# Router logits taken from the attention output by linearity, and the overflow test read from the softmax sums

## What is computed

```python
x = x + _L0_conv_ref(_gn(x), ...)        # linear attention, 8 heads of 32
t = t + _L1_attn_ref(_ln_t(t), ...)      # softmax attention, 8 heads of 32
t = t + _L1_ffn_ref(_ln_t(t), ...)       # experts chosen by a Sinkhorn router
# in _L1_attn_ref
scores = einsum('bhnd,bhmd->bhnm', q, k) / sqrt(Dh)
attn = softmax(scores, axis=-1)
out = einsum('bnd,ed->bne', sa, w_agg) + b_agg
# in _L1_ffn_ref, on batches folded to 4 x 4096 in shape only
gate_logits = einsum('bhnd,hde->bhne', xh, gate_weight)    # 8 numbers a token
gates = _sinkhorn(gate_logits)           # log(clip(logits, 1e-6)), 8 rounds
vals, idx = top_k(g_t, m)                # the best 128 tokens of each expert
```

## Time and profile before

| | us |
|---|---|
| median of 3 runs | 1469.12 |
| lowest, highest | 1467.42, 1470.44 |
| profiled execution, span from the first to the last instruction | 1467.7 |
| PE busy in it | 1339.3 |
| DVE busy | 1021.3 |
| ACT busy | 868.7 |
| POOL busy | 562.6 |

### The profile page before, as it was taken

One profiled execution on the slowest core, in us unless ns is written; L12 is line 12 of the kernel. 1 busy time (PEld: TensorE's weight loads), 2 busy tenths in 40 slices (PEclk: granted clock), 3 DMA queues, 4 the chain that ended last, 5 costly groups with the idle time before them and its releaser, 6 DMA issues.

```text
span 1467.7 us, 29142 instructions
## 1 busy us (share of the span) xinstructions
PE 1339.3 (91%) x10849; PEld 915.8 (62%) x10849; DVE 1021.3 (70%) x2114; ACT 868.7 (59%) x1268; POOL 562.6 (38%) x1068
## 2 busy tenths in 40 slices
PE   5789989999999999999999999999998999987535
PEld 3556656667576767676767676656666567766423
DVE  3536766858585857586768676787789776899771
ACT  2456557677667767677666767665675667542100
POOL 1132530445134513551245214520554116875443
PEclk9899989999999999999999999999999999999665
DMA  2051013600360037002710272005500265454322
GB/s 79 29 137 51 1 30 87 172 16 27 80 184 15 2 93 193 18 2 75 184 46 2 57 168 79 2 30 117 144 15 2 65 169 191 128 158 134 118 68 80
DMA packets 66785, 119.13 MB, mean 81 GB/s; under 512 B 10705, under 2 KB 46546, under 8 KB 66642
## 3 DMA queue, kind: packets, MB, share of 16 engines
q1 hardware_dynamic: 57682, 90.48, 22.9%
q0 software_dynamic: 8960, 26.75, 6.0%
HBM read 29.11 MB, written 33.55 MB: 43 GB/s over the span
## 4 chain that ended last, share of the span: by engine, by line
PE 62%; DVE 24%; issue 6%; POOL 4%; ACT 3%; DMA 0%; DVEq 0%; POOLq 0%; ACTq 0%
PE shared L938 30%; PE scores L894 12%; PE acc L916 11%; DVE prob_sum L1635 6%; PE acc L913 3%; PE shared L933 3%; DVE acc_sb L1609 2%; DVE bn L1344 2%; ACT probs L1209 2%; DVE work L1543 1%; PE acc L926 1%; DVE resid L1350 1%; DVE best_i L1541 1%; DVE best L1539 1%; DVE bn_x L1404 1%
## 5 line engine op out<-in xcount | busy, mean ns | idle before, releaser
L1209 ACT ACTIVATE probs<-scores 128x1024 f32<-128x1024 f32 x512 | 516.0, 1024 | 178.1 <-PE scores L894 94.0
L894 PE MATMUL scores<-query_stack,key_stack 96*128 96x256 f32 x2048 | 342.1, 308 | 16.0 <-ACT probs L1209 15.7
L1635 DVE TENSOR_TENSOR prob_sum<-prob_sum,probs 128x512 f32<-128x512 f32 x512 | 331.3, 707 | 0.0
L894 PEld LDWEIGHTS scores<-query_stack,key_stack 96*128 96x128 f32 x2048 | 275.9, 192 | 85.1 <-issue 39.1
L916 PE MATMUL acc<-probs,v_all 128*32 128x256 f32 x4096 | 289.2, 389 | 0.0
L1242 POOL TENSOR_TENSOR attn_T<-acc_sb 128x256 f32<-128x256 f32 x56 | 41.4, 740 | 447.8 <-DVE acc_sb L1609 445.0
L938 PE MATMUL shared<-w_sb,chan 128*128 128x512 f32 (+1 forms) x512 | 186.7, 501 | 5.9 <-DVE chan L1438 5.9
L916 PEld LDWEIGHTS acc<-probs,v_all 128*32 128x32 f32 x4096 | 114.8, 110 | 104.0 <-issue 37.9
L938 PEld LDWEIGHTS shared<-w_sb,chan 128*128 128x128 f32 x512 | 91.9, 192 | 62.5 <-issue 57.9
L938 PE MATMUL shared<-chan,w1T 128*128 128x512 f32 x256 | 121.3, 608 | 2.1 <-ACT chan L1125 2.1
L1635 DVE TENSOR_TENSOR prob_sum<-probs 128x512 f32<-128x512 f32 x128 | 98.4, 810 | 18.8 <-ACT probs L1209 16.5
(11 more groups left out here) (220 smaller groups left out, 2036.7 us busy)
## 6 DMA issues: line engine op xcount, KB each, us to landing
query_stack<-hi SPq DMA_DIRECT2D x120, 128.0 KB, 2.5
key_stack<-hi SPq DMA_DIRECT2D x120, 128.0 KB, 2.5
x_sb<-in_x_dram SPq DMA_DIRECT2D x8, 1024.0 KB, 5.3
out_dram<-resid SPq DMA_DIRECT2D x16, 512.0 KB, 4.8
tokens_scratch<-resid SPq DMA_DIRECT2D x16, 512.0 KB, 5.5
tokens_scratch<-rows SPq DMA_DIRECT2D x16, 512.0 KB, 3.3
key_stack<-lo SPq DMA_DIRECT2D x60, 128.0 KB, 2.5
query_stack<-lo SPq DMA_DIRECT2D x60, 128.0 KB, 2.5
```

Of the source, the lines that this page charges most:

```text
L894: last = pe.matmul(score_ps[u % 2][:, QB * r:QB * (r + 1)], key_stack[stack, HG * g + r, P * kt:P * (kt + 1)], query_stack[stack, HG * g + ...
L1209: act.activation(probs[:, u % PROBS, :], score_ps[u % 2][:, :], ACT.Exp, scale=DH ** -0.5) \
L1635: dve.tensor_tensor(total[:, part], probs[:, (u - 1) % PROBS, part] if kt == 1 else total[:, part], probs[:, u % PROBS, part], ALU.add).th ...
```

## The change

The logits are linear in what the layer norm takes in, so they are computed from its input and corrected. With r the scale of a token's norm and m its mean, a logit is r * (t G - m * sum(G)), G being the router's weights. t is the token before attention plus the attention's output plus the bias, and each part gives its share where it is already multiplied:
- `waggT` gets 8 more columns (w_agg times G, made once by `gate_weights`), so `agg` yields 264 columns; DVE adds the 8 to `gates` in a second operation;
- `w1T` gets 8 more columns (G), so `v` yields the share of the token before attention, from its normed rows; ACT copies the 8 columns apart, scaled by the token's deviation `ln_s`. `v` now makes one tile a bank, in 8 steps instead of 4;
- `deviations` and `means` (DVE, 3 and 1 operations of 128x8 to 128x64) and `logits` (DVE, 4 operations of 128x32, twice a batch) add the means and apply r and the clip;
- `z2T`, `gate`, `square` and `norms` are gone.

The overflow test reads the reciprocals of the softmax sums. POOL's `divide` sends them to `inverses` by a DMA (4 partitions of 256 numbers), for batch 7's blocks too, where POOL had nothing to do. `copy_acc` now also waits until the DMA of the block before it has landed. At the end DVE compares 128x512 numbers in three operations.

```diff
-             ("gvar",), ("store_stats", 1), ("z2T", 0), ("store_rows", 3), ("z2T", 1), ("z2T", 2), ("z2T", 3),
-             ("xn", 0), ("gate", 0), ("rest", 2), ("qk0", 0), ("gate", 1), ("store_rows", 4), ("qk0", 1), ("xn", 1),
+             ("gvar",), ("store_stats", 1), ("store_rows", 3), ("logits", 0), ("xn", 0), ("rest", 1.5),
+             ("qk0", 0), ("store_rows", 4), ("qk0", 1), ("xn", 1),
...
                 if kind == "agg":
...
-                    last = product(ps[:, 0:C], [(attn_T[:, c, tok[at[0]]], waggT[:, c, :]) for c in range(CH)])
+                    last = product(ps[:, 0:C + E], [(attn_T[:, c, tok[at[0]]], waggT[:, c, :]) for c in range(CH)])
...
                 elif kind == "v":
-                    for j in range(2):
-                        last = product(ps[:, C * j:C * (j + 1)],
-                                       [(chan[:, c, tok[2 * at[0] + j]], w1T[:, c, 2 * C:3 * C]) for c in range(CH)])
+                    last = product(ps[:, 0:C + E], [(chan[:, c, tok[at[0]]], w1T[:, c, 2 * C:3 * C + E])
+                                                    for c in range(CH)])
...
+                    act.activation(v_all[:, 0:G + 1:G, t, :], ps[:, 0:C].rearrange("p (g n) -> p g n", g=G), ACT.Copy)
+                    logits = gates[:, 0 if shifted_by_max else seg.front, t, :]
+                    read(act.activation(logits, ps[:, C:C + E], ACT.Copy, scale=ln_s[:, t:t + 1]), seg, *st)
...
             def copy_acc(blk):
                 act.wait_ge(s["blocks_done"], blk + 1)
                 await_count(act, "attn_ready", blk)
+                await_count(act, "inverses_in", 0 if shifted_by_max else 16 * blk)
...
             def divide(blk):
                 a, g, qb = blk // (G * NQB), blk % (G * NQB) // NQB, blk % NQB
-                if direct(blk):
-                    return
                 pool.wait_ge(s["recip_ready"], blk + 1)
...
+                if not shifted_by_max:
+                    row, half = HG * (blk % (P // HG)), blk // (P // HG)
+                    pool.dma_start(inverses[row:row + HG, half, :], acc_sb[0:P:DH, QB:2 * QB]).then_inc(s["inverses_in"], 16)
...
+                elif kind == "logits":
+                    dve.wait_ge(s["row_r_ready"], stored + at[0] + 1)
+                    part = slice(T // 2 * at[0], T // 2 * (at[0] + 1))
+                    logits, means = logits_of(seg.store)[:, part, :], mean_part[:, part, :]
+                    link(means_times_sums(means, part))
+                    link(dve.tensor_tensor(logits, logits, means, ALU.subtract))
+                    link(dve.tensor_tensor(logits, logits, ln_r[:, part].unsqueeze(2).to_broadcast([P, T // 2, E]),
+                                           ALU.mult))
+                    dve.tensor_scalar(logits, logits, CLIP, None, ALU.max).then_inc(s["logits_ready"], 1)
```

More of the change, by code:

```diff
@@ L86, in order @@
 def order(attend, front, store):
-    store_part = {"agg", "store_stats", "store_rows", "z2T", "gate"}
+    store_part = {"agg", "store_stats", "store_rows", "logits"}
     attend_part = {"resid"}
@@ L118, in first_order @@
 def first_order():
-    steps = [x for x in order(False, True, False) if x[0] not in ("zT", "proj", "v", "square", "norms")]
+    steps = [x for x in order(False, True, False) if x[0] not in ("zT", "proj", "v", "deviations", "means")]
     rows = [steps.index(("front_rows", t)) for t in range(T)]
@@ L644, in lay_out @@
         steps = order(seg.has("attend"), seg.has("front"), seg.has("store"))
-        if seg.deferred:
-            steps = sum(first_order(), [])
+        if seg.first:
+            steps = first_order()
         steps = [x for x in steps if x not in seg.early]
-        if shifted_by_max:
-            steps = [x for x in steps if x[0] not in ("square", "norms")]
-        elif seg.last:
-            steps = [("bound_rows",), *steps, ("bound",)]
-        seg.projections, seg.squares = ([x[1:] for x in steps if x[0] == kind] for kind in ("proj", "square"))
-        steps = [x for x in steps if x not in seg.deferred]
+        if seg.last:
+            steps = [*steps, ("bound_rows",), ("bound",)]
+        seg.projections = [x[1:] for x in steps if x[0] == "proj"]
         dealt = (PAIRS if seg.has("front") else PAIRS // 2) if seg.has("attend") else 1
@@ L697, in build_segments @@
     added = T - 1 - DIRECT
-    first_front = next((seg for seg in segments if seg.deferred), None)
+    first_front = next((seg for seg in segments if seg.first), None)
     first_queries_in = env["first_queries_in"]
@@ L951, in step @@
                     pe.wait_ge(s["attn_ready"], G * NQB * seg.stores + NQB * (G - 1) + at[0] // (QB // P) + 1)
-                    last = product(ps[:, 0:C], [(attn_T[:, c, tok[at[0]]], waggT[:, c, :]) for c in range(CH)])
-                elif kind == "z2T":
-                    pe.wait_ge(s["z2_ready"], T * seg.stores + at[0] + 1)
-                    last = transposes(ps, *(rows[:, at[0], half[c]] for c in range(CH)))
-                elif kind == "gate":
-                    await_read(pe, seg, "z2T", at[0])
-                    await_small(pe)
-                    last = product(ps[:, 0:E], [(z2T[:, c, tok[at[0]]], gate_w[:, c, :]) for c in range(CH)])
+                    if at[0] == 0 and first_front:
+                        await_read(pe, first_front, "gate_weights")
+                    last = product(ps[:, 0:C + E], [(attn_T[:, c, tok[at[0]]], waggT[:, c, :]) for c in range(CH)])
                 elif kind == "xT":
@@ L1009, in step @@
                     last = product(ps[:, 0:C], [(ones[0:1, :], env["bagg_row"])])
+                elif kind == "gate_weights":
+                    await_small(pe)
+                    pe.wait_ge(s["to_turn_in"], 48)
+                    for c in range(CH):
+                        last = product(ps[:, E * c:E * (c + 1)],
+                                       [(env["wagg_nat"][:, o, half[c]], gate_w[:, o, 0:E]) for o in range(CH)])
+                elif kind == "gate_sums":
+                    pe.wait_ge(s["gate_bias_ready"], 1)
+                    last = product(ps[:, 0:2 * E], [(ones[:, :], gate_w[:, c, :]) for c in range(CH)])
                 elif kind == "proj":
                     j, h = at
-                    if seg.deferred:
+                    if seg.first:
                         for n in range(2 * CH):
@@ L1034, in step @@
                     elif store_of:
-                        for t in range(T - 2, T):
-                            await_read(pe, store_of[routing.groups[g][1] - 1], "gate", t)
+                        pe.wait_ge(s["logits_ready"], 2 * (store_of[routing.groups[g][1] - 1].stores + 1))
                     else:
@@ L1281, in step @@
                         .then_inc(s["resid_ready"], 1)
-                elif kind == "head_stats" and not seg.deferred:
+                elif kind == "head_stats" and not seg.first:
                     pool.wait_ge(s["head_v_ready"], 2 * seg.fronts + at[0] + 1)
```

235 lines of the change are left out of this document (120 added, 115 removed), and 6 rows, old and new, of the table steps.

## The result

The changed kernel takes 1513.9 us (median of 4 runs, 1506.1 to 1515.8) against 1468.8 us: ratio 1.0303, 95% interval [1.027, 1.0337]. It is 3% slower. I had forecast 1448 us, with 1472 as the upper end.

The account below looks back on a forecast made before the run. PE was taken to bound the middle segments (149.22 of 149.9 us busy). Segment 1 -4.5, five segments -17.5, segment 7 -2.5, batch 7's attention +1.5, front +1, tail +1: -21.0 us, so 1448 us; range 1416 to 1472.

Parts of the forecast that it names:

- three signs of being wrong: Segments shrink by 8 us without a group norm gap; `acc_sb` waits for a DMA; a segment has several clock falls.
- PE's work taken out: Per middle segment, `gate`, `z2T` and `norms` matmuls go: 8.7 us together, net 8.3 us after 0.4 for added columns.
- The wait at the group norm: Per middle segment, PE waits between the group norm's two matmuls, now back to back: 1.05 us lost.
- The wait for `xn`: Between the second group norm matmul and the first `qk0`, PE waits for `xn`: 1.7 us, bounds 0 and 3.4.
- I add 0.4 us for these: Behind `xn` on DVE, the reciprocal and next slot's additions delay ACT's exponentials and PE's scores: 0.4 us a middle segment.
- The clock: One fall to half clock per middle segment, 3.4 us long, costing 1.7 us; bounds 0 and 3.4.
- Segment 7: 1022 to 1186 us: 8.3 us of PE work goes, but DVE's top-k and the waits leave a 2.5 us gain.
- Segment 1: No store part, 16 `norms` of two batches go (6.9 us), stalls stay: a gain of 4.5 us.
- The DMA: POOL's 64 DMAs of the reciprocals and the wait in `copy_acc` stay hidden: 0, upper bound 3 us a segment.
- Batch 7's attention: PE loses 5.3 us, but POOL's moved layer norm and three DMAs add 8.7: +1.5 us, bounds -5 and +9.
- The slowest that I worked out: Rival: late DMAs make `copy_acc` wait and PE stop, with second clock falls: 1488 us, half of it 1468; chance 0.13.
- of the higher bounds: Rival: waits of 3.4, 1.97 and 3.4 us a segment eat the middle segments' gain: 1468 us; chance 0.15.

Follow-up runs that it names:

- norms_out: The kernel before without its `square` and `norms` steps, overflow test reading a constant, every other step in its slot: 1446.84 us.
- gmean_apart: The changed kernel with the group norm's first matmul ahead of the last `agg`, so its two matmuls are apart again: 1509.62 us.
- rows_late: The changed kernel with the four normed rows of a batch's second half (`store_rows` 4 to 7) about one slot later: 1484.45 us.
- head_apart: The changed kernel with the head statistics and what follows them back in their old slots 12 to 18: 1487.46 us.
- layout_kept: The changed kernel with every shared step in its slot of the kernel before, removed steps kept as empty places: 1450.05 us.
- repaired: The changed kernel with rows_late, gmean_apart, head_apart and the router weights' products later in the front: 1453.85 us.
- best: layout_kept with the router weights' products later in the front and `store_rows` 4 to 7 one and a half slots later: 1442.05 us.
- kept_no_dma: layout_kept without the DMAs of the reciprocals and the wait for them, overflow test left out: 1440.29 us.
- best_no_dma: best without the DMAs of the reciprocals and the wait for them, overflow test left out: 1426.14 us.
- no_dma: The changed kernel without the DMAs of the reciprocals and the wait for them, overflow test left out: 1505.25 us.

## Why the prediction was wrong, step by step

Of the three signs of being wrong that the prediction named, two came: ACT's copies waited for the DMA, and most middle segments had more than one fall of the clock.

- **PE's work taken out: right.** Forecast 8.7 us of removed matmuls, measured 8.4. The added columns cost 0.8 instead of 0.4. `norms` was the term too high: 0.43 us each, read from one pitch, against a median of 0.34; norms_out gave 2.4 us a segment.
- **The wait at the group norm: right in place and size.** Forecast 1.05 us; PE waited 0.93 at the second matmul. What it cost the kernel is not shown: with it gone, in gmean_apart, a later wait of 0.76 us appeared, and the 4.3 us gained are inside the spread of the runs.
- **The wait for `xn`: right, 1.3 us against 1.7.** The chain from the second matmul to `xn` took the time read from the earlier trace rows.
- **The step that failed: "I add 0.4 us for these", all that the sum has for what stands behind the group norm's chain.** I followed that chain to the first `qk0` and stopped there. Behind the group norm's root on POOL stands `row_deviations`, 7.8 us, then `store_rows` 4 on ACT, then the exponentials, then PE: 3.16 us of stop. This path has no term in the sum. The diff and the orders said that `store_rows` 4 had come from the second half of slot 6 to the first, while `gvar` had gone from slot 3 to slot 4: three slots between them had become two. I priced a late layer norm only in batch 7's attention. rows_late shows the cost of it: 29.5 us. DVE's additions, which the 0.4 us were for, make an exponential wait 4.86 us (2.58 before), but they are not what stopped PE: in rows_late it waits 4.85 us for them all the same, and PE's stop is gone.
- **A second chain has no term either.** In slots 12 to 16 the head statistics moved by about a slot against POOL's products. No sentence of the prediction speaks of it; head_apart shows 26 us by the medians, 19 between the profiled executions.
- **The clock: the right direction, the size too small.** Forecast one fall of 3.4 us a middle segment, measured 3.4 to 10.2 us, mostly two falls, each behind a stop. In layout_kept, repaired and best, whose stops in the middle segments stay under 1.5 us, it never falls there. The length of a stop alone does not settle it: in the changed kernel the clock also fell behind the wait of 0.93 us at the group norm (at 754.08) and did not behind a stop of 1.69 us at `lo` (at 660). From segment 1 to segment 7 half clock rose from 34 to 75 us; half of the difference, 20 us of the 45, is an estimate of what it cost.
- **Segment 7: forecast -2.5, measured +7.9.** It has the same two stops, and 20.5 us of half clock instead of 6.8. layout_kept takes 158.9 there, 5.2 less than before.
- **Segment 1: forecast -4.5, measured -1.3.** norms_out and kept_no_dma reach 149.5 and 149.7; layout_kept, with the DMAs, 159.4. Between these profiles lie 17 us of half clock. That the DMAs set it off is not shown: best and best_no_dma take nearly the same time in segment 1 (154.9 and 155.3), and there the kernel with the DMAs has less half clock (10.2 us against 20.5). One profiled execution of each is little to go by: eleven executions of the kernel before, run beside these, had mean clocks of 0.947 to 0.960 and took 1460.0 to 1470.2 us.
- **The front: forecast +1, measured +6.** DVE's copy waited 3.74 us for PE with the head scaling behind it; moving the two steps gave 5.6 us back by the medians, 4.4 in the front itself. What stands in the queue behind a waiting instruction has to be named, on DVE, too.
- **The DMA: in this kernel nearly right, by luck.** I took 0 with 3 us a segment as the upper bound, and named a segment's first block as the tightest place, where my own rows had 3.3 us of issue and landing against 2.7 us of room. In the changed kernel the six waits of 15.4 us are at another block and hide a product that is late, and without the DMAs it takes 9 us less. In best, where the order is mended, the copy waits 1.8 to 4.1 us at just the place named, and the DMAs cost 16 us by the medians, 11 between the profiled executions. The 64 issues took 0.57 to 0.67 us each, and the median landing in best was 1.9 us, against the 0.50 and 2.5 of the earlier trace rows: the duration was right, the wait in front of the next copy was not.
- **The shared port.** The Trainium skill ("SBUF — State Buffer", section "SBUF: two separate sides") has a POOL operation that reads SBUF and a DVE operation with two inputs in SBUF lock each other out. That POOL's DMAs stand still it says of DVE's operations in a two-port mode; of `tensor_tensor`, the form of the additions, it infers that it leaves the writing of descriptors alone. So by this page the additions are no reason to fear for the DMAs of the reciprocals. Of the small operations the trace agrees: POOL's `row_deviations` takes 0.19 to 0.20 us an operation beside DVE's reciprocal, which has one input (448.2 to 449.3), and 0.51 to 0.52 beside the additions (450.2 to 454.2). The chain that ACT waits for is as long as before, though (7.8 us, 8.0 before), so the change did not lengthen it. For the DMA issues the trace agrees, too: beside the additions or not, none took over 0.67 us.
- **Batch 7's attention: +1.8 against +1.5, the wait named is there, its price comes with the DMAs.** The moved layer norm makes ACT wait:

```profile
1274.95 0.60 ACT L1096 ACTIVATE rows<-resid,ln_b,ln_r 128x256 f32<-128x256 f32 x1 [2.48 <-POOLq L1239]
```

In no_dma the layer norm stands behind the same nine gathers, ACT does not wait for it, and the stage takes 138.9 us, 0.9 less than before. So the moved chain alone made nothing slower; with DMAs of the reciprocals between POOL's steps the stage takes 2.7 us more.

- **The tail: +3.6 against +1.** It lies behind the last scatter, at the barrier that ends the main program. There POOL's queue has a DRAIN that the other engines wait for; its row in the kernel before and in the changed one (duration in ns, start in us):

```profile
L790 POOLq DRAIN  x1: 3323/3323/3323, 1459.1 to 1459.1; - x1
```

```profile
L778 POOLq DRAIN  x1: 6922/6922/6922, 1500.3 to 1500.3; - x1
```

It took 6.92 us in every kernel with the DMAs of the reciprocals, and 3.32 in the four others without them, no_dma, kept_no_dma, best_no_dma and norms_out. So the DMAs cost 3.6 us there in any order, and 3.6 of the 4.2 us between the tails of best and best_no_dma; why the drain takes longer is not shown.
- **The rivals.** The slowest that I worked out was 1488 us, built on the DMA. All the waits I listed "of the higher bounds" came to 1468. Both summed waits that I had found; neither asked how many chains had moved.

## What to carry to other kernels

When a planner deals fewer steps over the same slots, compare for every chain across engines (here matmul, POOL's root, ACT's normed rows) how many slots lie between its ends before and after, and not only for the chains that the edit touches. Removed work was also cover: here 8 us less of it on PE came with 13 us of stops and slow clock. To separate the two, keep the removed steps as empty places first, time that, and only then move.

A transfer that looks free beside a late product is priced again when the product is on time.

## What the runs showed that I had not expected

A stop of 3.2 us on PE is followed by the clock at 0.50 (1.2 GHz) for 3.4 us here, and in head_apart for 6.8 us behind the same stop; in layout_kept, whose stops are under 1 us there, 727 us in a row passed at the full clock. So the stop of 3.2 us costs some 1.7 us more by the clock behind it, half of the 3.4 (an estimate). And the same matmuls in the same slots of segment 1 took 149.7 and 159.4 us in two kernels that differ in a DMA of 4 KB a block, with 6.8 and 23.9 us of half clock, and nearly the same in two other kernels that differ in the same way. And the end of the program was 3.6 us longer with those DMAs, by one DRAIN on POOL's queue that no sum had.
